# Box sums of the max/average chain: from TensorE to accumulating transfers issued by GpSimd, with level 0 one image ahead

## Time and profile before

| | us |
|---|---|
| median of 3 runs | 1402.02 |
| the profiled execution's own time | 1402.31 |
| its span | 1400.3 |
| TensorE busy | 1256.5 (90%) |
| VectorE busy | 1177.1 (84%) |
| ScalarE busy | 727.6 (52%) |
| GpSimd busy | 162.5 (12%) |
| start of `rstd` in steps 1 to 8 | 377.6, 513.6, 650.3, 787.1, 923.8, 1060.5, 1197.0, 1317.0 |

### The profile page before, as it was taken

The page is one execution under the profiler, slowest core; times in us unless marked ns, Lnnn a source line. Parts: engine busy times, 40 slices in busy tenths (PEclk is TensorE's granted clock), DMA queues, the critical chain, the costliest instruction groups (busy, mean ns, idle before and its releaser), DMA issues.

```text
span 1400.3 us, 18688 instructions
## 1 busy us (share of the span) xinstructions
PE 1256.5 (90%) x7290; PEld 1090.6 (78%) x7290; DVE 1177.1 (84%) x1241; ACT 727.6 (52%) x787; POOL 162.5 (12%) x77
## 2 busy tenths in 40 slices
PE   3569898849899999999999999999999999999697
PEld 1249898738779888988898889878988888898597
DVE  7779898898999799979998998899989988985443
ACT  0246767653475366636653655465447543753342
POOL 1567767300000000000000000000000000000000
PEclk9869999979999999999999999999999999999899
DMA  7401212110000200020002000200020011001000
GB/s 282 165 30 76 91 76 106 76 60 30 0 16 1 102 14 5 15 90 15 0 15 90 15 0 15 90 15 0 15 90 15 0 37 69 0 1 60 0 1 30
DMA packets 19319, 63.37 MB, mean 45 GB/s; under 512 B 1616, under 2 KB 4304, under 8 KB 19280
## 3 DMA queue, kind: packets, MB, share of 16 engines
q1 hardware_dynamic: 18576, 62.53, 12.0%
q10 hardware_dynamic: 704, 0.30, 0.1%
HBM read 37.13 MB, written 25.17 MB: 44 GB/s over the span
## 4 chain that ended last, share of the span: by engine, by line
PE 34%; issue 26%; DVE 17%; ACT 3%; DVEq 0%; POOL 0%; POOLq 0%; ACTq 0%
PE slot L1203 11%; PE slot L1150 8%; PE ps_level L1203 8%; DVE between L1488 4%; PE slot L1219 3%; DVE a L1488 2%; PE slot L575 2%; PE slot L1190 1%; DVE f_all L307 1%; DVE x L1531 1%; DVE work_b L230 1%; DVE q_all L307 1%; DVE pt_all L249 1%; DVE pt_all L1526 1%; PE ps_level L1235 1%
## 5 line engine op out<-in xcount | busy, mean ns | idle before, releaser
L1203 PE MATMUL slot<-f_all,q_all 128*128 128x512 f32 x768 | 197.1, 409 | 13.4 <-ACT pooled L1343 13.4
L1203 PE MATMUL ps_level<-v_all,pt_all 128*128 128x256 f32 x1536 | 201.5, 288 | 5.4 <-ACT mixed L1362 5.2
L1203 PEld LDWEIGHTS ps_level<-v_all,pt_all 128*128 128x128 f32 x1536 | 191.0, 194 | 7.7 <-DVE pt_all L1492 5.4
L1203 PEld LDWEIGHTS slot<-f_all,q_all 128*128 128x128 f32 x768 | 145.9, 196 | 44.1 <-ACT pooled L1343 14.8
L1488 DVE SCALAR_TENSOR_TENSOR a<-between,k_columns,a 128x992 f32<-128x992 f32 (+1 forms) x128 | 157.5, 1232 | 5.5 <-ACT a L1334 3.2
L1082 POOL TENSOR_TENSOR c_rstd<-c_spread,k_minus_half 128x2 f32<-128x2 f32 x8 | 5.6, 699 | 1052.9 <-DVE gmean L1565 1052.9
L1492 DVE TENSOR_TENSOR pt_all<-slot,pt_all 128x1024 fp32r<-128x1024 f32 x64 | 78.1, 1221 | 47.7 <-ACT pt_all L1348 47.7
L1357 ACT CAST v_all<-y 128x1024 fp32r<-128x1024 f32 x32 | 33.7, 1053 | 159.4 <-DVE y L1521 159.3
L1362 ACT ACTIVATE mixed<-ps_level,row_inv 128x256 f32<-128x256 f32 x64 | 30.3, 473 | 153.9 <-PE ps_level L1203 153.9
L1334 ACT ACTIVATE a<-between,k_columns 128x1024 f32<-128x1024 f32 x64 | 79.4, 1240 | 30.8 <-DVE between L1488 29.8
L1497 DVE TENSOR_REDUCE c_minus_max<-slot 128x1 f32<-128x1024 f32 x64 | 78.1, 1220 | 11.5 <-PE slot L1203 11.5
(11 more groups left out here) (185 smaller groups left out, 2824.5 us busy)
## 6 DMA issues: line engine op xcount, KB each, us to landing
levels<-x_all SPq DMA_DIRECT2D x32, 512.0 KB, 2.6
x_all<-in_x SPq DMA_DIRECT2D x8, 1024.0 KB, 13.1
f_all<-levels SPq DMA_DIRECT2D x8, 1024.0 KB, 4.9
x<-in_x SPq DMA_DIRECT2D x8, 1024.0 KB, 4.9
out<-x SPq DMA_DIRECT2D x8, 1024.0 KB, 4.0
pooled<-levels SPq DMA_DIRECT2D x8, 512.0 KB, 3.3
wide<-levels SPq DMA_DIRECT2D x7, 512.0 KB, 3.3
x_all<-in_w_c SPq DMA_DIRECT2D x2, 512.0 KB, 3.8
```

The source lines that it names most:

```text
L1203: last = nc.tensor.matmul(out, lhs, rhs, start=(n == 0), stop=(n == len(parts) - 1))
```

## The change

In steps 0 to 6 TensorE, `zt_hi`, `zt_lo` and `turn_level`, `box_level`, `level_hi`, `level_lo` no longer take part in the chain. A level now lies in SBUF with rows of 34 elements (`PITCH`: 32 and two zeros), 32 rows are 1088 elements (`ROWS`), and its 5x5 box sum is made by transfers between SBUF tensors that GpSimd issues, most with `accum_op=ALU.add` (destination = destination + source), shifted by 1, 2 or 3 elements for the sums along a row and by whole rows for the sums along a column. `add_round` has eight rounds, and each waits for the one before: round 0 copies the level to `boxes` (for level 0 also to `twos`; for levels 1 and 2 ScalarE makes that copy, `begin_twos`); round 1 makes sums of two; rounds 2 and 3 add these twice to `boxes`; round 4 copies `boxes` to `twos`; round 5 makes sums of two rows; rounds 6 and 7 add these. A step issues 25 such transfers of about 0.56 MB.

The sums and the maxima of level 0 are made one image ahead: step i makes those of image i + 2 (`ahead`), `level_mixture(0)` of image i + 1 stands at t = 2 of the attention, `level_mixture(1)` where `level_mixture(0)` was, and the mixture of level 2 at the beginning of the next step. GpSimd's list in step i is `rstd` of image i - 1, levels 1 and 2 of image i + 1, level 0 of image i + 2. Level 0 of image 1 is made by GpSimd in the last eight turns of `phase_b`. `x_aux` of the next image for cv2 and cv1 gets a load of its own after c1 (`load_own`), and the order of the four inputs of cv2 changes.

The loop now has steps 1 to 5; step 6 stands by itself without `ahead`. The diff, cut to its core:

```diff
-        self.wide = sb("wide", [P, LEVELS + 1, N])
+        self.middle = sb("middle", [P, LEVELS - 1, 2 + ROWS])
+        self.last = sb("last", [P, N])
+        self.ahead = sb("ahead", [P, 2 + ROWS])
+        self.twos = sb("twos", [P, (H + 4) * W])
+        self.boxes = sb("boxes", [P, H * WP])
+        self.ahead_boxes = sb("ahead_boxes", [P, PITCH + ROWS])
...
-        self.first_in = counted("first_in", 16)
+        self.ahead_in = counted("ahead_in", 16, -16)
...
-        self.done = counted("done", MIX * LEVELS)
+        self.first_max = counted("first_max", MIX - 1)
+        self.done = counted("done", 1 + MIX * (LEVELS - 1))
...
+        self.twos_begun = counted("twos_begun", LEVELS - 1, 1 - LEVELS)
+        self.twos_in = counted("twos_in", 16, -16)
+        self.boxes_in = counted("boxes_in", 16 * LEVELS, -16 * LEVELS)
+        self.rows_added = counted("rows_added", 48 * LEVELS, -48 * LEVELS)
+        self.rows_copied = counted("rows_copied", 16 * LEVELS, -16 * LEVELS)
+        self.columns_added = counted("columns_added", 48 * LEVELS, -48 * LEVELS)
...
+    def begin_twos(self, act, i, level):
+
+        wait(act, self.done, i, ready(level))
+        self.nc.scalar.copy(self.twos[:, PITCH - 2:PITCH + ROWS], self.middle[:, level - 1]).then_inc(self.twos_begun.sem, 1)
+
+    def waited(self, pool, sig, i, k):
+        wait(pool, sig, i, k)
+        pool.sem_inc(self.gate, 1)
+
+    def add_round(self, pool, i, level, n):
+
+        source, boxes = (self.middle[:, level - 1], self.boxes) if level else (self.ahead, self.ahead_boxes)
+        twos, before = self.twos, 48 * level
+        if n == 0 and level:
+            self.waited(pool, self.done, i, ready(level))
+        elif n == 0:
+            self.waited(pool, self.ahead_in, i, 16)
+            pool.dma_start(twos[:, PITCH - 2:PITCH + ROWS], source[:, :]).then_inc(self.twos_in.sem, 16)
+        if n == 0:
+            pool.dma_start(boxes[:, PITCH:PITCH + ROWS], source[:, 2:2 + ROWS]).then_inc(self.boxes_in.sem, 16)
+        elif n == 1:
+            if level:
+                self.waited(pool, self.twos_begun, i, level)
+            else:
+                self.waited(pool, self.twos_in, i, 16)
+            pool.dma_start(twos[:, PITCH - 2:PITCH + ROWS - 1], source[:, 1:2 + ROWS],
+                           accum_op=ALU.add).then_inc(self.rows_added.sem, 16)
+        elif n == 2:
+            self.waited(pool, self.boxes_in, i, 16 * level + 16)
+            self.waited(pool, self.rows_added, i, before + 16)
+            pool.dma_start(boxes[:, PITCH:PITCH + ROWS - 2], twos[:, PITCH - 2:PITCH + ROWS - 4],
+                           accum_op=ALU.add).then_inc(self.rows_added.sem, 16)
+        elif n == 3:
+            self.waited(pool, self.rows_added, i, before + 32)
+            pool.dma_start(boxes[:, PITCH:PITCH + ROWS - 2], twos[:, PITCH + 1:PITCH + ROWS - 1],
+                           accum_op=ALU.add).then_inc(self.rows_added.sem, 16)
+        elif n == 4:
+            self.waited(pool, self.rows_added, i, before + 48)
+            pool.dma_start(twos[:, 0:PITCH + ROWS], boxes[:, 0:PITCH + ROWS]).then_inc(self.rows_copied.sem, 16)
+        elif n == 5:
+            self.waited(pool, self.rows_copied, i, 16 * level + 16)
+            pool.dma_start(twos[:, 0:ROWS], boxes[:, PITCH:PITCH + ROWS],
+                           accum_op=ALU.add).then_inc(self.columns_added.sem, 16)
+        elif n == 6:
+            self.waited(pool, self.columns_added, i, before + 16)
+            pool.dma_start(boxes[:, 2 * PITCH:PITCH + ROWS], twos[:, 0:ROWS - PITCH],
+                           accum_op=ALU.add).then_inc(self.columns_added.sem, 16)
+        else:
+            self.waited(pool, self.columns_added, i, before + 32)
+            pool.dma_start(boxes[:, PITCH:ROWS], twos[:, 2 * PITCH:PITCH + ROWS],
+                           accum_op=ALU.add).then_inc(self.columns_added.sem, 16)
...
+    def add_level(self, pool, i, level):
+        for n in range(ROUNDS):
+            self.add_round(pool, i, level, n)
...
+    def mixture_of_added(self, dve, i, level):
+        wait(dve, self.columns_added, i, 48 * level + 48)
+        boxes = self.boxes if level else self.ahead_boxes
+        self.mixture(dve, i, level, padded2d(boxes[:, PITCH:PITCH + ROWS]), self.work_b if level else self.early)
...
-    ORDER = (0, 2, 1, 3)
+    ORDER = (2, 0, 1, 3)
...
+    def load_own(self, sp, i):
+        sp.dma_start(self.lo(0).bitcast(F32), self.levels[i, :, 0]).then_inc(self.own_in.sem, 16)
...
+                    chain.clear_rows_above(pool)
+                if s >= 2 * B:
+                    chain.add_round(pool, 1, 0, s - 2 * B)
...
-TURN_AT, BOX_AT = 1, TILES - 2
+MIX_AT = 2
...
-            step(0, True, False, True)
-            with eng.Fori(1, B - 1) as i:
-                step(i, True, True, True)
...
+            step(0, True, False, True, True)
+            with eng.Fori(1, B - 2) as i:
+                step(i, True, True, True, True)
+            step(B - 2, True, True, True, False)
+            step(B - 1, True, True, False, False)
+            step(B, False, True, False, False)
...
-            def step(i, conv, attn, chained):
+            def step(i, conv, attn, chained, ahead):
+                if ahead:
+                    chain.waited(sp, chain.first_max, i + 1, 2)
+                    chain.waited(sp, chain.boxes_in, i + 1, 16)
+                    chain.waited(sp, chain.rows_added, i + 1, 16)
+                    chain.load_ahead(sp, i + 2, levels)
...
-                    wait(sp, cv, i, 2 * CT)
-                    load_chain(i + 1)
                     if attn:
-                        wait(sp, turned, i - 1, TILES)
+                        chain.waited(sp, turned, i - 1, TILES)
+                    else:
+                        wait(sp, cv, i, 2 * CT)
                     pooled.load_second(sp, i + 1)
...
-                    wait(sp, c1, i, KT)
+                    chain.waited(sp, c1, i, KT)
+                    pooled.load_own(sp, i + 1)
                     pooled.load_others(sp, i + 1)
...
-            def step(i, conv, attn, chained):
+            def step(i, conv, attn, chained, ahead):
                 if attn:
...
+                if chained:
+                    chain.add_level(pool, i + 1, 1)
+                    chain.add_level(pool, i + 1, 2)
+                if ahead:
+                    chain.waited(pool, chain.columns_added, i + 1, 48 * LEVELS)
+                    chain.add_level(pool, i + 2, 0)
...
-                        if chained and t == TURN_AT:
-                            turn_level(0)
-                        if chained and t == BOX_AT:
-                            box_level(0)
...
+                if conv and attn:
+                    chain.level_split_hi(act, i, LEVELS)
...
+                        if n == 1:
+                            chain.begin_twos(act, i + 1, 1)
...
-                        if chained and t == TURN_AT + 1:
-                            level_hi(0)
+                        if chained and t == MIX_AT + 1:
+                            chain.begin_twos(act, i + 1, 1)
...
+                if chained:
+                    chain.begin_twos(act, i + 1, 2)
...
-                        if chained and attn and m == 0:
-                            level_hi(2)
                         if chained and m == 0:
-                            pooled.split_hi(act, i + 1, 2)
-                            pooled.split_hi(act, i + 1, 3)
-                        if chained and not attn and m == 1:
-                            level_hi(2)
+                            for n in range(1, KT):
+                                pooled.split_hi(act, i + 1, n)
                 if chained:
-                    for level in range(1, KT):
+                    for level in range(1, LEVELS):
                         chain.level_split_hi(act, i + 1, level)
...
                 def level_mixture(level):
-                    chain.mixture_of_boxes(dve, i, level, slots_of["zb", level][:, :])
+                    chain.mixture_of_added(dve, i + 1, level)
...
+                def ahead_maxima(*at):
+                    if at[0] == 0:
+                        wait(dve, chain.done, i + 1, MIX)
+                    chain.maxima(dve, i + 2, 0, *at, first=chain.inner_ahead())
...
+                if conv and attn:
+                    chain.level_split_lo(dve, i, LEVELS - 1)
+                    chain.mixture_of_added(dve, i, LEVELS - 1)
...
-                    for level in range(2, KT):
-                        chain.level_split_lo(dve, i, level)
+                    chain.level_split_lo(dve, i, LEVELS)
...
+                    level_mixture(0)
...
+                            if n >= KT * STAGES - MIX + 1:
+                                level_maxima(1, n - KT * STAGES + MIX - 1)
...
-                        if chained and t == TURN_AT + 1:
-                            level_lo(0)
-                        if chained and 0 < t < TILES - 1:
```

(58 more changed lines are left out.)

218 lines of the change are left out of this document (79 added, 139 removed).

## The result

The changed kernel takes **1588.22 us** (median of 4 runs, 1582.0 to 1595.74) where the kernel before takes 1400.76 in the runs beside it: a ratio of **1.135, 95% interval 1.131 to 1.139**, 13% slower. The profiled execution took 1595.74 us, with a span of 1593.9; it is the slowest of the four, 7.5 us above their median. The prediction said 1520 with a range of 1405 to 1650.

What follows compares the result with a forecast made beforehand. TensorE sets the loop now; afterwards the next `rstd`, behind all rounds on GpSimd's queue, would. 1402 + 94 + 33 - 10.7 + 3 = 1521.6, stated as 1520 us, range 1405 to 1650.

Steps and rivals of the forecast that it cites:

- rival B: Loop: rounds from about 5.0 us make level 1 late, so `level_mixture(1)` waits; 1654 us, or about 1790; chance 27%.
- The price of a round: GpSimd's transfers, issue to issue: copy 3.65 us, addition 5.25 us, fourteen rounds 68.5 us, mean 4.9 us.
- rival A: Loop: short rounds stay hidden and TensorE's 11.5 us gain shows; faster below a 3.5 us mean, 1385 or 1341; chance 12%.
- step 6: Last chained step: no level 0 issued, so 126 us instead of 136.5, -10.7 us.
- steps 7, 8 and the end: Final steps: no chain before or after, so a change of 0.
- The loop's period: Between `rstd` starts in steps 1 to 6: 155.5 us instead of 136.7, +94 us over five intervals.
- the 3.0 and 5.4 us: TensorE's gains ahead of `level_mixture(0)` (3.0 us) and `level_mixture(1)` (5.4 us), which bring these mixtures earlier.
- Step 0: Before the loop: `level_mixture(1)` ends at 340, `rstd` of step 1 comes at 410.8 instead of 377.56, +33 us.
- the 3 us for `phase_b`: End of `phase_b`: eight rounds on GpSimd each add an issue and a wait for the former transfer, +3 us.
- The clock: TensorE restarts at 1.2 GHz after its long pause, some 5 us before it waits for VectorE; 1 us kept.
- Level 1: Seven dependent rounds from 47 us end at 82 us, just before the mixture needing them at 82.5; cost 0.
- 87 + 14 d: Loop period in us: 83.7 + 1.3 + 14 d + 1 + 1, d the mean round, unless 126 is more.

## Why the prediction was right in kind and short in size

**The mechanism held.** The prediction put the loss in one place, the next `rstd` behind all rounds of a step on GpSimd's queue, with `c_shift`, the normalisation and the q, k, v products behind it. The waits show it there, and no other of that size in the compute engines' loop, up to 33.4 us a time at `c_shift` and 27.5 at TensorE, and the two ways of taking that wait away bring back all 190 us. The sizes did not hold as well. `c_shift` was to wait 20 to 30 us, the `rstd` to lie 150 to 160 us apart, and they lie 166.3 to 167.7 apart. The time lies inside the stated range, but above the 1460 to 1560 us that had the largest chance. Of the rivals only B lies above 1560, and its mechanism, level 1 late, is not what made the time so.

**The price of a round held.** Predicted: an adding round 5.25 us, a copy 3.65. Measured undisturbed: 5.2 and 3.5. The closeness is partly luck, since no row showed such a transfer and the price was put together from loads of like size and 0.35 us for issuing. The Trainium skill (Collectives: The Full Stack, "The bandwidth ceiling") gives, for the adding transfers of a collective, the second source read and not the add as what makes them slow; the difference of 1.7 us between the two versions of the same transfers agrees with it in direction, though no run here separates the read from the add. Its formula for GpSimd's transfers (DMA: Bandwidth & Descriptors, "Anatomy of one DMA"), 3.3 us here, is near the copy's 3.5 us; rival A, which took such a price for all rounds, falls with the additions.

**The sum fell short by 74 us** in the profiled execution (1595.74 against 1521.6), by 67 against the median. By its terms:

| | predicted us | measured us |
|---|---|---|
| start of `rstd` in step 1 against before, `phase_b` included | +36 | +46.9 |
| five intervals of the loop | +94 | +151.7 |
| step 6 | -10.7 | -3.5 |
| steps 7, 8 and the end | 0 | -1.5 |

- **The loop's period**, 155.5 predicted, 166.3 measured in the interval shown. Two terms are off. First, `level_mixture(1)` was to end at 83.7 us and 1 us for the clock was to come on top, 84.7; level 2's first copy is issued 88.5 us after the mark (424.47 to 512.99). Most of the 3.0 and 5.4 us that TensorE was to gain by then did not arrive. In the version without transfers this mixture starts 86.1 us after the mark, in the kernel before the instruction in its place 86.7, and in the 85.3 us up to it VectorE is busy for 80.5: as I read it, its own work fills that part. In this first interval 0.9 us more are its wait for level 1. This is the sentence "VectorE loses three low parts ... still below TensorE": it compared busy sums, and the version without transfers puts the floor at 131.5 us and not at 126. Second, the fourteen rounds were to take 68.5 us (11 x 5.25 + 3 x 3.65 is 68.7, rounded down) and take 76.0 (514.28 to 555.44, and 555.44 to 590.25). At 5.2 and 3.5 they would be 67.7; the other 8.3 us are longer rounds, which the prediction did not have at all. 4.6 of them are in the copy beside `load_others`, and those are shown to come from the loads; the longer additions stand beside the image's load and beside `load_ahead`, and their cause was not tried. The two, +3.8 and +7.5, less 0.4 for the quick hand-over to `rstd`, make the 10.8 us.
- **Step 0** is 11 us later than reckoned. The same loads, issued at 359.90 and 360.27, stand beside its rounds too: the one issued at 361.70 takes 8.9 us, and 5.3 with the loads cut; the fourteen take 72.9 us and not 68.5. And the row of fourteen begins at 351.06, where the prediction had 344.3 with the 3 us for `phase_b`. Most of this belongs to this one execution and not to the change. The version with the power left out has the same instructions up to there, and issues the same round 5.4 us earlier (changed kernel first):

```profile
351.06 0.84 POOL L220 DMA_DIRECT2D twos<-middle  x1 [0.55 <-ACT twos L198]
...
345.65 0.85 POOL L220 DMA_DIRECT2D twos<-middle  x1 [0.55 <-ACT twos L198]
```

  The first low part of stage three starts at 277.87 in the changed kernel and at 271.31 there; before it starts at 267.28. So the 3 us for `phase_b` were not far off, and a single profile can't price that term more closely.
- **Step 6** gained 3.5 us and not 10.7: again the floor of 131.5 to 133, not 126.
- **The clock** was right in size. TensorE idles for 27.5 us and starts again at 430.38. The changed kernel by busy time from `rstd` to the first score product (columns as above):

```profile
430.30:436.50 6.20, 3.08 (x6) 2.00 (x7) 6.17 (x6) 4.55 (x5) 0.00 (x0) 0.50 0.01 1
436.50:440.00 3.50, 3.50 (x11) 2.80 (x10) 3.43 (x4) 2.08 (x2) 0.00 (x0) 0.59 0.02 5
440.00:447.60 7.60, 7.60 (x58) 7.19 (x57) 7.53 (x8) 6.67 (x7) 0.00 (x0) 1.00 0.00 0
```

  The granted clock is 0.50, the lower level of 1.2 GHz, until VectorE's low part comes, and full from about 440 on. The score product starts 23.1 us after `rstd`, in the kernel before 22.0: about the 1 us kept for it.
- **Level 1** did not delay the loop. In the first interval two of its rounds took 7.6 us each, for a reason that was not tried; its rounds ended 86 us after the mark, and `level_mixture(1)` waited 0.9 us for them. That is rival B's wait, and it comes this once. In the other steps the rounds ended at 82 us as forecast, some 5 us before the mixture, which was later than the forecast's 82.5.

**Rival A's point of decision was nearly right.** It had the kernel faster from a mean round of 3.5 us down. With the measured terms the loop breaks even where 88.5 + 1.3 + 14 d + 0.6 for the hand-over equals 136.7, at a mean of 3.3 us with the stretched rounds counted in, an estimate. If 5 us of stretching stay, undisturbed rounds would have to take 3.0. The run with copies alone has undisturbed rounds of 3.5 us but a mean of 4.2, for which the prediction's 87 + 14 d gives 146 us; the loop took 148.

## What to carry to other kernels

On a queue that runs in order, an instruction of 1 us that the other engines need must not stand behind a chain of dependent transfers: look where that queue is idle and put the chain there. Here the same transfers cost some 190 us against the kernel before in one place and nothing in another. An average share of busy DMA engines says little on a single transfer: 0.47 over the step, 0.99 around the one that took longest. When an edit takes work off the bounding engine, its gain ends at the next engine and earlier than the busy sums say: with busy sums of 124 and 120 us the step took 131.5.

## What the runs showed of the hardware

- An adding transfer between SBUF tensors of 0.54 MB lands in 4.5 to 4.7 us in the changed kernel and the same transfer without adding in 2.9 to 3.6; end to end in a dependent row 5.2 against 3.5 us. GpSimd spends 0.85 us to issue the first kind and 0.55 the second.
- A transfer issued by GpSimd 2 us behind 1.5 MB of loads from SP's queue took 8.1 us in place of 3.5, and 3.8 with the loads cut to 0.1 MB. The DMA share was 0.99 in those 7 us, though 0.47 over the step.
- 4096 rows of 128 B took twice as long to land as 128 rows of 4 KB (7.6 against 3.7 us for 512 KB), and yet the adding transfer beside them took 6.7 us with either.
